# Block-causal attention with a routed feed-forward on one core: row maxima of several heads in one VectorE instruction, the diagonal mask on TensorE, and a tail transposed by VectorE

## The reference, cut to what matters

```python
xn = layernorm(x)
# attention: 16 heads; the projection of 1024 x 768 is *reshaped* to (16, 1024, 48), so that a head
# owns 64 consecutive tokens and its 1024 rows are those tokens' 16 pieces of 48 numbers
q, k, v = split((xn @ W_qkv + b_qkv).reshape(4, 16, 1024, 48), 3)         # 16 numbers each
attn = softmax(q @ k.T * scale + triu(-inf, 1))
attention = (attn @ v).reshape(4, 1024, 256) @ W_out + b_out
# feed-forward: light for all tokens, heavy for 256 tokens of each batch
light = gelu(rms_norm(xn) * gamma_l @ w1_l + b1_l) @ w2_l + b2_l          # hidden 128
s = xn @ routing_token                       # 50 rounds of coordinate descent, then top 256 by score
heavy = gelu(rms_norm(xn[chosen]) * gamma_h @ w1_h + b1_h) @ w2_h + b2_h  # hidden 1024, times a gate
out = x + attention + light + scatter(heavy)
```

## Time and profile before

| | us |
|---|---|
| runs: median (lowest, highest) | 711.55 (711.24, 713.2) |
| the profiled execution | 714.09 |
| its span, first to last instruction | 712.4 |
| TensorE busy, share of the span | 667.8 (94%) |
| VectorE busy | 554.8 (78%) |
| ScalarE, GpSimd busy | 403.5 (57%), 380.6 (53%) |

### The profile page before, as it was taken

The page is one execution under the profiler, slowest core; times in us unless marked ns, Lnnn a source line. Parts: engine busy times, 40 slices in busy tenths (PEclk is TensorE's granted clock), DMA queues, the critical chain, the costliest instruction groups (busy, mean ns, idle before and its releaser), DMA issues. The chain is left out here.

```text
span 712.4 us, 12474 instructions
## 1 busy us (share of the span) xinstructions
PE 667.8 (94%) x3987; PEld 296.2 (42%) x3987; DVE 554.8 (78%) x1571; ACT 403.5 (57%) x908; POOL 380.6 (53%) x774
## 2 busy tenths in 40 slices
PE   4997999899999999899989999999999999999995
PEld 2653555333323333233323332333333436568665
DVE  4865888999999999999989999999998575152111
ACT  2332222787777777467768877777767554332320
POOL 4686130488775847857957853554442454413303
PEclk9999999999999999979999999999999999999998
DMA  8888996678949649696987944844833323442512
GB/s 276 207 219 196 242 264 179 154 141 129 180 70 161 129 63 163 103 132 111 152 160 99 164 73 52 120 75 51 174 63 29 121 60 92 147 148 88 119 59 30
DMA packets 247057, 92.49 MB, mean 130 GB/s; under 512 B 212992, under 2 KB 232608, under 8 KB 243872
## 3 DMA queue, kind: packets, MB, share of 16 engines
q1 hardware_dynamic: 245456, 89.60, 63.0%
q0 software_dynamic: 1536, 2.10, 1.8%
HBM read 56.65 MB, written 35.01 MB: 129 GB/s over the span
## 5 line engine op out<-in xcount | busy, mean ns | idle before, releaser
L1288 DVE CUSTOM_DVE_ANT_0 ps<-ps,maskrow 128x640 f32<-128x640 f32 (+7 forms) x512 | 375.3, 779 | 30.9 <-PE ps L1039 29.4
L897 ACT ACTIVATE strips<-ps 128x512 f32<-128x512 f32 (+1 forms) x608 | 313.2, 576 | 112.0 <-PE ps L1081 89.5
L1039 PE MATMUL ps<-QTk,QTq 96*128 96x512 bf16 (+3 forms) x768 | 189.2, 335 | 18.5 <-DVE mx L1288 10.6
L1081 PE MATMUL ps<-QTq,QTk 99*128 99x512 bf16 (+3 forms) x768 | 185.4, 331 | 2.8 <-DMA QTq<-m_d 1.9
L1099 PE MATMUL ps<-strips,vext 128*32 128x512 f32 (+3 forms) x1536 | 162.8, 500 | 0.9 <-DVE oT L1311 0.4
L1039 PEld LDWEIGHTS ps<-QTk,QTq 96*128 96x128 bf16 x768 | 53.3, 98 | 166.6 <-DVE mx L1288 133.1
L1081 PEld LDWEIGHTS ps<-QTq,QTk 99*128 99x128 bf16 x768 | 68.2, 98 | 89.3 <-ACT strips L897 41.2
L1739 POOL TENSOR_SCALAR_AFFINE_SELECT strips<-strips 128x512 f32<-128x512 f32 x128 | 79.3, 636 | 43.2 <-ACT strips L897 42.8
L999 PE MATMUL ps<-shared,xrT 128*128 128x384 f32 (+1 forms) x256 | 94.8, 503 | 0.2
L1288 DVE DVE_READ_ACCUMULATOR2_ANT mx<- 128x1 f32 x512 | 72.1, 141 | 0.0
L999 PEld LDWEIGHTS ps<-shared,xrT 128*128 128x128 f32 x256 | 47.3, 196 | 26.8 <-issue 3.1
(11 more groups left out here) (153 smaller groups left out, 689.8 us busy)
## 6 DMA issues: line engine op xcount, KB each, us to landing
pieces_d<-pieces SPq DMA_DIRECT2D x64, 192.0 KB, 3.4
qk<-qkv_d SPq DMA_DIRECT2D x64, 128.0 KB, 4.0
qkv_d<-shared SPq DMA_DIRECT2D x16, 384.0 KB, 3.8
QTq<-pieces_d SPq DMA_DIRECT2D x16, 384.0 KB, 5.2
QTk<-pieces_d SPq DMA_DIRECT2D x16, 384.0 KB, 7.7
vext<-qkv_d SPq DMA_DIRECT2D x16, 256.0 KB, 5.8
QTq<-pieces_d SPq DMA_DIRECT2D x16, 256.0 KB, 5.6
QTk<-pieces_d SPq DMA_DIRECT2D x16, 256.0 KB, 8.3
```

Of the source, the lines that this page charges most:

```text
L897: nc.scalar.activation(dst, src, ACT.Exp, scale=SCALE).then_inc(exp_done, 1)
L1039: mm = pe.matmul(psM[:, s, at:at + n], QTq[0:W, f % 3, c * 1024 + qb * P:c * 1024 + (qb + 1) * P], QTk[0:W, f % 3, c * 1024 + k0:c * 1024 ...
L1081: mm = pe.matmul(psE[:, (NE * q + j) % ES, k * n:(k + 1) * n], QTk[0:W + 3, q % 3, c * 1024 + kb * P:c * 1024 + (kb + 1) * P], QTq[0:W + 3 ...
L1288: ins = nc.vector.tensor_tensor_reduce(scores, scores, maskrow[:, 1024 - n:1024], 1.0, MASKED, ALU.add, ALU.max, mx[:, f % 2, 8 * c + qb:8 ...
```

## The change

It does five things.

- **Units of C.** A unit is now a block of queries of one, two or four heads: blocks 7 to 4 of one head each, blocks 3 and 2 for two heads at once, blocks 1 and 0 for all four, 22 units for a step. For one head VectorE's instruction is as before. For several heads it is one `tensor_reduce` (maximum) over all of them, and the mask is added before by TensorE: a product of a bfloat16 identity (`eye`) with a bfloat16 mask block, accumulated onto the last 128 columns of each head. `BEGUN` is 14.
- **Constants.** GpSimd makes `eye` and `mask` (`N_CONST` 16), and TensorE waits for all constants behind its second tile.
- **Front.** SP's loads stand at other tiles, VectorE's transposes behind tiles 5, 13, 18.
- **Tail.** `load_sa` writes 64-column blocks to 32-partition groups, with four DMAs of 256 B runs for a unit; VectorE turns 32 x 32 blocks (`turned`, two instructions for a unit) into `saT`, which has a buffer for each u. TensorE's transposes and ScalarE's copies are gone. W_out's rows are loaded in the order that results. `project_c` has four PSUM banks. The heavy bias is multiplied by the gate ahead, and a heavy row takes one instruction.
- **Planner.** Costs, due times and constants are other ones.

```diff
+UNITS = [((c,), qb) for c in range(4) for qb in (7, 6, 5, 4)]
+UNITS[4:4] = [((0, 1), 3), ((0, 1), 2)]
+UNITS[10:10] = [((0, 1, 2, 3), 1), ((0, 1, 2, 3), 0)]
+UNITS[16:16] = [((2, 3), 3), ((2, 3), 2)]
-EARLY, BEGUN = 3, 12
+EARLY, BEGUN = 3, 14
-STEP, PACE = 29.60, 29.94
-SOON, LATER, BEHIND = 0.15, 8.0, 1.44
+STEP, PACE = 29.32, 30.56
+SOON, LATER, BEHIND = 0.10, 17.9, 2.02
-    T_AT = {5: 0, 10: 1, 15: 2}
+    T_AT = {5: 0, 13: 1, 18: 2}
-    N_DCONST, N_CONST, N_FOLD = 2, 14, 5
+    N_DCONST, N_CONST, N_FOLD, N_WD = 2, 16, 5, 10
-        psC = ps[:, 4:6]
+        psC = [ps[:, b] for b in (0, 1, 4, 5)]
...
-                if t in (2, 5, 11, 16):
-                    load_qk((2, 5, 11, 16).index(t))
-                elif t in (4, 13):
-                    load_v(t // 10)
-                elif t == 20:
+                if t in (2, 10, 14, 20):
+                    load_qk((2, 10, 14, 20).index(t))
+                elif t in (26, 27):
+                    load_v((26, 27).index(t))
+                elif t == 16:
                     load_light()
-                elif t in (6, 15, 22):
+                elif t in (6, 17, 23):
...
+                elif t == 8:
+                    load_pieces(0, 0)
+                    load_pieces(0, 1)
+                elif t in (19, 24):
+                    load_pieces((19, 24).index(t) + 1, 0)
+                elif t in (21, 25):
+                    load_pieces((21, 25).index(t) + 1, 1)
...
             def load_sa(i, u):
-                sp.dma_start(sa_in[:, u], sb3[...]).then_inc(c_in[u], 16)
+                for a in range(4):
+                    sp.dma_start(sa_in[32 * a:32 * a + 32, u].rearrange("p t e -> p (t e)").rearrange("p (m f) -> p m f", m=16),
+                                 sa_blocks[2 * i + u, a]).then_inc(c_in[u], 16)
...
         @block.tensor
...
+            pe.wait_ge(consts, N_CONST)
+
             def ring_item(item):
...
+                    w = (qb + 1) * P
+                    for k, c in enumerate(heads):
+                        ...  (one matmul for each 512 keys, stop only if one head)
+                    if len(heads) > 1:
+                        a_bank = 512 // w
+                        for k in range(0, len(heads), a_bank):
+                            n = min(a_bank, len(heads) - k)
+                            at = head_at(u, k)
+                            last = psM[:, s, at:at + n * w].rearrange("p (k n) -> p k n", k=n)[:, :, w - P:w]
+                            mm = pe.matmul(last, eye[:, :], mask[:, :, :].to_broadcast([P, n, P]), start=False, stop=True, ...)
...
-            def transposes_c(i, u, t):
...
         @block.vector
+                if len(heads) == 1:
+                    ins = nc.vector.tensor_tensor_reduce(scores, scores, maskrow[:, 1024 - n:1024], 1.0, MASKED, ALU.add, ALU.max, ...)
+                else:
+                    ins = nc.vector.tensor_reduce(mx[...][:, heads[0]:heads[-1] + 1, qb], scores, AX.X, ALU.max)
...
+            def turned(i, u):
+                dve.wait_ge(c_in[u], 16 * 4 * (i + 1))
+                if i > 0:
+                    dve.wait_ge(o_ps, 8 * (i - 1) + 4 * u + 4)
+                elif u > 0:
+                    dve.wait_ge(qk_ps, NE * NQ)
+                blocks = sa_in[:, u].rearrange("p t e -> p (t e)").rearrange("p (m k f) -> p k m f", k=KE, f=32)
+                for k in range(KE):
+                    nc.vector.transpose(saT[u][:, k, :].rearrange("p (m s) -> p m s", s=32), blocks[:, k]).then_inc(saT_done, 1)
+            last_outputs = ("OT", NQ - 1, 1)
             for item in order["Vector"]:
+                if item == last_outputs:
+                    turned(0, 0)
+                    turned(0, 1)
...
-                    nc.vector.tensor_tensor(hv[:, st, :], psH[:, st % 2, 0:E], bias_h, ALU.add).then_inc(hv_half, 1)
-                    nc.vector.tensor_scalar(hv[:, st, :], hv[:, st, :], gw[:, st:st + 1], None, ALU.mult).then_inc(hv_done, 1)
+                    nc.vector.scalar_tensor_tensor(out=hv[:, st, :], in0=psH[:, st % 2, 0:E], scalar=gw[:, st:st + 1],
+                                                   in1=hv[:, st, :], op0=ALU.mult, op1=ALU.add).then_inc(hv_done, 1)
...
         @block.gpsimd
             const(pool.tensor_copy(tokid[:, :, :], tokid_i[:, :, :]))
+            const(pool.tensor_copy(eye[:, :], ident[:, :]))
+            const(pool.tensor_copy(mask[:, 0, :], maskrow[:, 1024 - P:1024]))
             group(3)
```

More of the change, by code:

```diff
@@ L103, in schedule @@
     chains = {
-        ("Tensor", "C"): [("C", f, c, u) for f in range(1, STEPS) for c in range(4) for u in range(NU)][BEGUN:],
+        ("Tensor", "C"): [("C", f, u) for f in range(1, STEPS) for u in range(NU)][BEGUN:],
         ("Tensor", "E"): [("E", q, j) for q in range(STEPS) for j in range(NE)],
@@ L113, in schedule @@
         ("Vector", "TP"): [("TP", f) for f in range(EARLY, STEPS)],
-        ("Vector", "C"): [("C", f, c, u) for f in range(1, STEPS) for c in range(4) for u in range(NU)][BEGUN:],
+        ("Vector", "C"): [("C", f, u) for f in range(1, STEPS) for u in range(NU)][BEGUN:],
         ("Vector", "MXT"): [("MXT", f) for f in range(1, STEPS)],
@@ L268, in ready @@
             return done.get(("landed", ("S_OUT",)))
[L269 removed]
+        return 11.17 * PACE
     def due(engine, x):
@@ L306, in takes @@
         if kind == "C":
-            widths = [(qb + 1) * P for qb in UNITS[x[3]]]
-            return sum(product_time(n) if engine == "Tensor" else 0.117 + n / 960 for n in widths)
+            heads, n = len(UNITS[x[2]][0]), (UNITS[x[2]][1] + 1) * P
+            if engine == "Tensor":
+                return heads * product_time(n) + (0.1 + 0.03 * heads if heads > 1 else 0.0)
+            return 0.117 + heads * n / 960
         if kind == "PV":
@@ L926, in hidden @@
                 nc.scalar.activation(hT[:, u, :], xrT[:, 0, 512 * (2 * i + u):512 * (2 * i + u) + 512], ACT.Gelu, bias=b1l[:, 0:1]).then_inc(h_done, 1)
-            def unit(i, u, more=True):
-                for t in range(4):
-                    n = 8 * i + 4 * u + t
-                    act.wait_ge(saT_ps, n + 1)
-                    if not (isinstance(i, int) and n < 2):
-                        act.wait_ge(o_ps, n - 1)
-                    nc.scalar.activation(saT[:, t % 2, :], psX[:, t % 2, 0:KE * P], ACT.Copy).then_inc(saT_done, 1)
-                    if t == 1 and more:
-                        hidden(i if u == 0 else i + 1, 1 - u)
             def gathered(h):
@@ L1122, in _, with project_c @@
                     ring_item(item)
[L1125 removed]
+            def project_c(i, u, t):
                 n = 8 * i + 4 * u + t
+                o = psC[n % 4][:, 0:E]
                 if t == 0:
[L1128 to L1132 removed]
+                    pe.wait_ge(h_done, 2 * i + u + 1)
+                if n == 0:
                     for x in slots[-MS:]:
@@ L1218, in _ @@
             heavy_hidden(1, range(4, NHC))
-            unit(3, 1, more=False)
+            unit(3, 1)
             heavy_out(1, range(4))
@@ L1549, in _ @@
             unit(1, 1)
+            turned(2, 1)
             dve.wait_ge(gs_done, 1)
@@ L1554, in _ @@
             dve.wait_ge(gu_done, 2 * NSLOT + 3)
+            heavy_bias(range(4))
             heavy_rows(range(2))
             unit(2, 0)
+            turned(3, 0)
             heavy_rows(range(2, 4))
             unit(2, 1)
+            turned(3, 1)
+            heavy_bias(range(4, NSLOT))
             unit(3, 0)
```

173 lines of the change are left out of this document (82 added, 91 removed).

## The result

The changed kernel takes 708.34 us (median of six runs, 706.49 to 708.65) where the kernel before took 711.82 beside it: ratio 0.9944, 95% interval 0.9927 to 0.996. That is 0.6% faster: little, but the interval leaves out 1. By the medians the gain is 3.5 us; the forecast was 6.5 (705 from 711.55). The two profiled executions lie nearer to the sum: 708.6 us against 714.1, 5.5 less, forecast 6.7. The sum is nearly right, two of its three terms are not. I mark three points in both traces: the first score matmul (E) of group 0 on TensorE, the end of the last product (PV), the end of the span.

The account below looks back on a forecast made before the run. VectorE was taken to pace C in the main loop, TensorE second by about 6%. Front +6, loop -3 and tail -9.7 made -6.7 us: 707.4 from the profiled 714.1, median forecast 705 us, range 692 to 715.

Parts of the forecast that it names:

- three terms: Whole kernel: front +6 us, main loop -3 us, tail -9.7 us, together -6.7 us.
- Edit 3: Front: TensorE's wait for all constants stalls it 5.4 us, slow clock behind costs 1.7, together 7.1 us.
- Edit 4: Front's loads: emptier queue brings the first pieces 1.3 us earlier, less slow clock 0.8; step 1's operands covered.
- The moved blocks and masks: Front: score blocks begun earlier and their masks add 0.4 us through VectorE and 1.3 through TensorE.
- Edit 1: Maxima of several heads: ten fewer VectorE instructions a step at 0.11 us each, 15.8 us over 14.35 steps.
- Edit 2: Main loop: masks on TensorE cost 0.9 us a step, 11.5 us net; with fewer waits, -3 us.
- second rival: C in the main loop: masks make TensorE the bound, loop pays 11.5 us in full, total 720; chance 0.13.
- the term set against it: Main loop: TensorE's waits for late VectorE vanish, 14.5 us, three quarters of 19, at least 8.9.
- first rival: Main loop: VectorE's gain comes through in full, loop -12 us, total 695; chance 0.18.
- Edit 5: Tail: TensorE's transposes and waits for copies go, -9.7 us (-10.5 to -5).
- third rival: Tail: turned rows come late, six units wait 1 to 2 us each, tail -2, total 712.5; chance 0.05.
- The marks: Signs set ahead: third tile near 24.5 us, later first C, VectorE some 92%, weight loads not waiting, tail some 101.5 us.

Follow-up runs that it names:

- constants late: TensorE's wait for all constants moved to just before the first score block, against the changed kernel: 702.28 us, 0.9861 of the kernel before.

## Why the prediction was right, and where it was not

*The sum* came near by luck: two errors of opposite sign, each near ten us, cancelled, front 10.5 too low, loop 9.7 too high. By the medians half of the forecast gain came, 3.5 us of 6.5.

*Edit 3* (7.1 us): right in place, mechanism (a stall of 5.2 us with a granted clock of 0.55 behind it) and nearly in size; undone, 6.3 us come back.

*Edit 4* is the step that failed. I credited a shorter queue ahead of the first pieces with 1.3 + 0.8 us and called the rest covered; I followed each load to the piece that TensorE needs, and not the load of group 1's rows, now behind the pieces, to the transpose that VectorE has at tile 13 ahead of the maxima. Undoing the order gives back 5.8 us. The credit itself is at most small: between the new order and the old the first C moves from 57.1 to 57.6 us (constants late) and from 63.9 to 65.4 (not late), which one profile does not tell from nothing. The moved blocks and masks, 1.7 us in my sum, are bounded by the 3.9 that remain, of which up to 1.7 are the clock; the rest I couldn't split.

*Edit 1*: a reduction's fixed part is 0.04 to 0.07 us, not 0.11. What VectorE sheds is well sized: 17.4 us of busy time less than with the masked instructions of the kernel before (419.8 to 402.4), where the working had 15.8; 8.3 of them are the number of instructions (410.7 when split). But that number pays little by itself: split again, the reductions cost the loop 0.7 to 2.5 us.

*Edit 2*: the masks cost 7.5 to 8.9 us, where the working had 12.9 (its 11.5 is less the 1.1 of columns moved, and 0.3 too low as a sum), so the second rival's mechanism is real. Its condition did not hold, since more waits vanished. What mattered is the term set against it, 14.5 us of waits. From masks on VectorE to none the loop gains 14.2 (457.5 to 443.3), of which 9.1 show as idle time on TensorE: the term came out as sized, though its three quarters were chosen and not derived. The other 7.4 us of the loop's 12.7 come between the kernel before and that kernel, which has the same 16 masked reductions a group, so neither grouping nor masks made it. The columns begun in the front are 1.1 of it and TensorE's idle time 1.2 (15.5 and 14.3 us); the 17 us at half clock, gone there, are worth some 7.6. Together that is more than 7.4, so some 2.5 us were lost elsewhere, which no run splits. By elimination this is the new units with their order, which I had given 5 us each way without looking at the clock in the loop. The first rival's number (-12) was met, but its mechanism, VectorE's gain in full, is not what made it: grouping and masks together are 5.3 to 6.7 of it.

*Edit 5*: right, -9.3 for -9.7, and alone -10.2. TensorE nowhere waits for `saT`; its waits in the tail come to 2.6 us (3.3 before). The third rival's late rows did occur once, without harm to TensorE:

```profile
615.51 1.30 DVE L1465 STREAM_TRANSPOSE QTq<-QTq 128x512 f32<-128x512 f32 x2 [4.48 <-DMA QTq<-sa_d]
```

*The marks* that I set: the third tile, the first C, VectorE's share and the tail came as told; the weight loads still wait (63.3 us for the masked maxima and 16.6 for the reductions in the loop, 122.5 before); and "a loop that gets shorter by over 10" was named as what would show the working wrong, and the loop did.

What stays open: how units and order share in keeping the loop off the half clock. With the new units, the old numbers' order brought 10 us at half back; with the old units, the new numbers did worse than the old ones. So it is the pair that counts, and no run here has the same order with both sets of units.

## What to carry to other kernels

When a load is moved in a queue, follow it to every in-order queue that waits for it, and ask what stands behind that wait: here one transpose held back the maxima that TensorE needed. Where two engines are each within a few per cent of the bound, an edit that shifts work between them is worth little (5.3 to 6.7 us here), while the order decided by 9.0 to 17.6; after any edit that touches a planned order, judge the order by the clock of each stretch and by the count and length of waits. Measure the parts of a combined change singly: here one part alone was worth three times the whole.

## What the runs showed of the hardware that was not expected

Waits do not price alike. With the masks on VectorE, 31 waits of at most 0.8 us, 10.0 us in all, left the clock of the loop at 2.4 GHz throughout; in the kernel before, 20 waits of up to 1.1 us, 8.9 in all, came with 17 us at 1.2 GHz, the longest stretch beginning amid three waits of 0.45 to 1.12 us within 4 us. This is seen in one execution of the first; its five others have a lower mean granted clock (0.988 to 0.993, 0.996 in the profiled one), so it need not hold in each.

And four row loads whose issue took SP 2.75 us took it 8.05 us behind the loads of the pieces; in the kernel before 2.82 and 8.38.
